# Rounding and clipping by a signed-byte write in the quantised feed-forward of a gated cross-attention block

## The reference

```python
def _act_fake_quant(x, clip_factor):
    scale = sigmoid(clip_factor) * max(abs(x)) / 127
    return clip(round(x / scale), -128, 127) * scale

xq = _act_fake_quant(layernorm(x), clip_x)
h  = _act_fake_quant(silu(xq @ Wg.T) * (xq @ Wu.T), clip_down)
x  = x + tanh(g_ffn) * (h @ Wd.T)          # Wg, Wu, Wd rounded by rows in the same manner
```

## Time and profile before

| | |
|---|---|
| median of 3 runs | 256.78 us (256.52 to 256.97) |
| span of the profiled execution, first to last instruction | 255.8 us; no time of its own is shown for this execution |
| median less span | 0.95 us, what lies around the span |
| PE busy | 212.0 us (83%), 1661 instructions |
| DVE busy | 217.3 us (85%), 447 instructions |
| ACT busy | 163.1 us (64%), 300 instructions |
| POOL busy | 137.8 us (54%), 241 instructions |
| granted TensorE clock, mean | 0.964 of full speed |

### The profile page before, as it was taken

The page is one execution under the profiler, slowest core; times in us unless marked ns, Lnnn a source line. Parts: engine busy times, 40 slices in busy tenths (PEclk is TensorE's granted clock), DMA queues, the critical chain, the costliest instruction groups (busy, mean ns, idle before and its releaser), DMA issues.

```text
span 255.8 us, 5381 instructions
## 1 busy us (share of the span) xinstructions
PE 212.0 (83%) x1661; PEld 144.3 (56%) x1664; DVE 217.3 (85%) x447; ACT 163.1 (64%) x300; POOL 137.8 (54%) x241
## 2 busy tenths in 40 slices
PE   0899999979989999999999999988672979846860
PEld 0688888857746666666656666644341433314640
DVE  3377799979898998989989898969977999999991
ACT  2246666475687766666677766677664778839920
POOL 7445568643452536284774848388835533320671
PEclk9999999999999999999999999999995899995996
DMA  6998959999446444355445252000003200000594
GB/s 221 236 293 285 295 142 233 275 256 256 133 151 165 141 110 104 95 118 128 125 111 136 55 136 64 4 0 4 1 0 108 100 1 0 0 1 0 65 137 133
DMA packets 34185, 30.80 MB, mean 120 GB/s; under 512 B 5232, under 2 KB 27760, under 8 KB 34160
## 3 DMA queue, kind: packets, MB, share of 16 engines
q1 hardware_dynamic: 29776, 27.74, 39.7%
q0 software_dynamic: 1360, 1.31, 4.2%
q10 hardware_dynamic: 3024, 1.44, 2.1%
HBM read 20.65 MB, written 9.70 MB: 119 GB/s over the span
## 4 chain that ended last, share of the span: by engine, by line
PE 34%; DVE 30%; issue 10%; ACT 7%; POOL 7%; DMA 5%; SPq 4%; POOLq 0%; ACTq 0%; DVEq 0%
PE bank_o L1466 9%; PE bank_a L1449 6%; PE bank_b L1435 4%; DVE h_max L1212 3%; PE bank_a L1475 3%; DVE arena L1248 3%; ACT arena L763 3%; DMA big<-in_ctx 3%; DVE big L1221 3%; PE bank_a L1352 3%; DMA big<-max_parts 2%; DVE arena L903 2%; DVE arena L1254 2%; DVE v_all L1270 2%; POOL big L485 1%
## 5 line engine op out<-in xcount | busy, mean ns | idle before, releaser
L913 DVE TENSOR_REDUCE neg_max<-bank_b 128x2 f32<-128x512 f32 x128 | 80.2, 673 | 4.9 <-PE bank_b L1341 3.0
L1449 PE MATMUL bank_a<-big 98*128 98x256 bf16 x256 | 48.9, 274 | 6.3 <-ACT arena L763 2.3
L763 ACT ACTIVATE arena<-bank_a 128x512 f32<-128x512 f32 x64 | 34.3, 605 | 13.9 <-PE bank_a L1449 13.8
L1435 PE MATMUL bank_b<-big 96*128 96x256 bf16 x224 | 42.7, 272 | 0.3 <-issue 0.2
L763 ACT ACTIVATE big<-bank_a 128x512 f32<-128x512 f32 x64 | 33.9, 595 | 12.3 <-PE bank_a L1449 12.1
L1449 PEld LDWEIGHTS bank_a<-big 98*128 98x128 bf16 x256 | 20.1, 97 | 25.5 <-issue 8.8
L1352 PE MATMUL bank_a<-arena,w_t 128*128 128x256 f32 x128 | 32.3, 401 | 0.2 <-issue 0.2
L1352 PEld LDWEIGHTS bank_a<-arena,w_t 128*128 128x128 f32 x128 | 24.7, 202 | 4.0 <-issue 0.6
L509 POOL TENSOR_TENSOR arena<-resid,arena 128x512 bf16<-128x512 f32 x16 | 18.4, 1163 | 10.9 <-ACT arena L701 10.9
L1435 PEld LDWEIGHTS bank_b<-big 96*128 96x128 bf16 x224 | 21.1, 97 | 4.5 <-issue 0.8
L569 POOL TENSOR_TENSOR x_rows<-x_rows,arena 128x256 f32<-128x256 f32 x14 | 11.6, 834 | 15.4 <-ACT arena L772 15.4
(11 more groups left out here) (179 smaller groups left out, 444.4 us busy)
## 6 DMA issues: line engine op xcount, KB each, us to landing
qk_parts<-arena SPq DMA_DIRECT2D x8, 768.0 KB, 4.9
big<-qk_parts SPq DMA_DIRECT2D x32, 192.0 KB, 3.2
big<-qk_parts SPq DMA_DIRECT2D x32, 128.0 KB, 3.2
x_rows<-in_x SPq DMA_DIRECT2D x8, 256.0 KB, 6.5
big<-qk_parts SPq DMA_DIRECT2D x32, 64.0 KB, 3.5
big<-in_ctx SPq DMA_DIRECT2D x7, 256.0 KB, 5.1
out<-x_rows SPq DMA_DIRECT2D x7, 256.0 KB, 2.8
out<-v_all POOLq DMA_DIRECT2D x5, 256.0 KB, 4.7
```

What stands on the lines that cost most here:

```text
L763: act.activation(probabilities(h), ring_bank(b, ("exp", h)).rearrange("p (c s) -> p c s", c=QC), ACT.Exp, scale=SCALE).then_inc(exp_done, 1)
L913: dve.tensor_reduce(neg_max[:, p, :, h], bank.rearrange("p (c s) -> p c s", c=QC), axis=AX.X, op=ALU.max, negate=True).then_inc(max_done, 1)
L1435: done = mm(to, q_st[0:KR, p, h, c * P:(c + 1) * P], k_st[0:KR, p, h], start=True, stop=not masked)
L1449: done = mm(to, k_st[0:KM, p, h, k * P:(k + 1) * P], q_st[0:KM, p, h], start=True, stop=not masked)
```

## The change

A write of an f32 value as a signed byte rounds it and holds it within -128 and 127. The change multiplies by the inverse scale and writes signed bytes, and a second instruction copies the bytes into bf16. The constant MAGIC, its removal and both clips go away for x and for h; the weights keep theirs. The byte buffers take a quarter of the room, so `x_int` holds all four chunks and `h_int` all eight batches, and the waits for a free buffer go away. ACT rounds h in one instruction of 128 x 768 (tile 1) and seven of 128 x 1536 (batches 1 to 7), where there were 15 of 128 x 768, and DVE copies h in two instructions of 128 x 768 and seven of 128 x 1536. The instructions before and after:

```diff
-                pool.tensor_scalar(xq[:, n % 2].rearrange("p t e -> p (t e)"), hats(n), INV_X, MAGIC, ALU.mult, ALU.add
+                pool.tensor_scalar(x_int[:, n].rearrange("p t e -> p (t e)"), hats(n), INV_X, 0.0, ALU.mult, ALU.add
                                    ).then_inc(pool_x, 1)
...
             over_scale(2)
-            pool.wait_ge(xq_ready, 3)
             over_scale(3)
...
-            act.activation(xq[:, 0, 2:4], v_all[:, 2:4], ACT.Identity, scale=INV_X, bias=magic[:]
-                           ).then_inc(x_over_scale, 1)
+            act.activation(x_int[:, 0, 2:4], v_all[:, 2:4], ACT.Copy, scale=INV_X).then_inc(x_over_scale, 1)
...
-            for t in range(1, T // P):
-                act.wait_ge(y_free, t + 1)
-                act.activation(h_round[:, t % CT], h_all[:, :, t * P:(t + 1) * P], ACT.Identity,
-                               scale=INV_H, bias=magic[:]).then_inc(y_rounded, 1)
+            act.activation(h_int[:, 0, :, P:S], h_all[:, :, P:S], ACT.Copy, scale=INV_H).then_inc(h_int_ready, 1)
+            for b in range(1, B):
+                act.activation(h_int[:, b], h_all[:, :, b * S:(b + 1) * S], ACT.Copy, scale=INV_H
+                               ).then_inc(h_int_ready, 1)
...
-            def rounded(to, rows):
-                chain.then(dve.tensor_scalar(to, rows, -MAGIC, QMAX, ALU.add, ALU.min))
-
-            def clip(to):
-                chain.wait()
-                dve.tensor_scalar(to, to, -QMAX - 1, None, ALU.max).then_inc(xq_ready, 1)
+            def whole_x(n, t=slice(0, CT)):
+                dve.tensor_copy(xq_b[:, n, t], x_int[:, n, t]).then_inc(xq_ready, 1)
 
             def quantise_ahead():
                 for n in (2, 3):
                     dve.wait_ge(pool_x, n - 1)
-                    rounded(xq_b[:, n - 1], xq[:, n % 2])
-                chain.wait()
-                for n in (2, 3):
-                    clip(xq_b[:, n - 1])
-
-            chain.step(dve.tensor_scalar(xq[:, 0, 0:2], v_all[:, 0:2], INV_X, MAGIC, ALU.mult, ALU.add))
-            rounded(xq_b[:, 0, 0:2], xq[:, 0, 0:2])
-            clip(xq_b[:, 0, 0:2])
+                    whole_x(n)
+
+            chain.step(dve.tensor_scalar(x_int[:, 0, 0:2], v_all[:, 0:2], INV_X, None, ALU.mult))
+            whole_x(0, slice(0, 2))
+            chain.step(dve.tensor_scalar(w_scale_x[:], w_scale[:, 0:2 * IC], S_X, None, ALU.mult))
             dve.wait_ge(x_over_scale, 1)
-            rounded(xq_b[:, 0, 2:4], xq[:, 0, 2:4])
-            chain.then(dve.tensor_scalar(w_scale_x[:], w_scale[:, 0:2 * IC], S_X, None, ALU.mult))
-            clip(xq_b[:, 0, 2:4])
-            chain.step(dve.tensor_scalar(xq[:, 1].rearrange("p t e -> p (t e)"), hats(1), INV_X, MAGIC, ALU.mult, ALU.add))
-            dve.wait_ge(xq_tr, 2)
-            rounded(xq_b[:, 0], xq[:, 1])
-            clip(xq_b[:, 0])
+            whole_x(0, slice(2, 4))
+            chain.step(dve.tensor_scalar(x_int[:, 1].rearrange("p t e -> p (t e)"), hats(1), INV_X, None, ALU.mult))
+            whole_x(1)
             dve.wait_ge(pad_zero, 2)
...
-            chain.step(dve.tensor_scalar(h_round[:, 0], h_all[:, :, 0:P], INV_H, MAGIC, ALU.mult, ALU.add))
+            chain.step(dve.tensor_scalar(h_int[:, 0, :, 0:P], h_all[:, :, 0:P], INV_H, None, ALU.mult))
+            dve.tensor_copy(hq[:, :, 0:P], h_int[:, 0, :, 0:P]).then_inc(hq_ready, 1)
+
             def whole(b):
-
-                def round_tile(i):
-                    if i:
-                        dve.wait_ge(y_rounded, i)
-                    dve.tensor_scalar(hq[:, :, i * P:(i + 1) * P], h_round[:, i % CT], -MAGIC, None, ALU.add
-                                      ).then_inc(y_free, 1)
-
-                def clip_tile(i):
-                    t = slice(i * P, (i + 1) * P)
-                    dve.wait_ge(y_free, i + CT + 1)
-                    dve.tensor_scalar(hq[:, :, t], hq[:, :, t], QMAX, -QMAX - 1, ALU.min, ALU.max
-                                      ).then_inc(hq_ready, 1)
-
-                i = b * QC
-                round_tile(i)
-                if b == 0:
-                    clip_tile(i)
-                round_tile(i + 1)
-                if b:
-                    clip_tile(i)
-                clip_tile(i + 1)
+                dve.wait_ge(h_int_ready, b + 1)
+                t = slice(b * S + (P if b == 0 else 0), (b + 1) * S)
+                dve.tensor_copy(hq[:, :, t], h_int[:, b, :, P if b == 0 else 0:S]).then_inc(hq_ready, 1)
...
                 def down_tile(b, c, to):
-                    pe.wait_ge(hq_ready, b * QC + c + 1)
+                    pe.wait_ge(hq_ready, b + 2 if b else c + 1)
```

More of the change, by code:

```diff
@@ L28 @@
 U8 = mybir.dt.uint8
+I8 = mybir.dt.int8
 MAGIC = 12582912.0
@@ L216, in flamingo_block @@
         p_second = part(HH * QC * S).rearrange("p (h c s) -> p h c s", h=HH, c=QC)
-        xq = part(2 * CT * E, True).rearrange("p (a t e) -> p a t e", a=2, t=CT)
-        xq_b = part(3 * CT * E // 2).bitcast(BF16).rearrange("p (a t e) -> p a t e", a=3, t=CT)
+        x_int = part(NCH * CT * E // 4, True).bitcast(I8).rearrange("p (a t e) -> p a t e", a=NCH, t=CT)
+        xq_b = part(NCH * CT * E // 2).bitcast(BF16).rearrange("p (a t e) -> p a t e", a=NCH, t=CT)
         xq_t = part(EC * T // 2).bitcast(BF16).rearrange("p (c t) -> p c t", c=EC)
@@ L222, in flamingo_block @@
         up_scaled = part(CW)
-        h_round = wgu_rows[:].rearrange("p g c e -> p (g c e)").rearrange(
-            "p (a c t) -> p a c t", a=CT, c=IC)
+        h_int = wgu_rows[:].rearrange("p g c e -> p (g c e)").bitcast(I8).rearrange(
+            "p (b c t) -> p b c t", b=B, c=IC)
         hq = part(IC * T // 2, True).bitcast(BF16).rearrange("p (c t) -> p c t", c=IC)
@@ L282, in flamingo_block @@
         pad_zero, h_scale_ready = sem("pad_zero"), sem("h_scale_ready")
-        y_rounded, y_free, hq_ready = sem("y_rounded"), sem("y_free"), sem("hq_ready")
+        h_int_ready, hq_ready = sem("h_int_ready"), sem("hq_ready")
         down_done, y_scaled, x2_stored = sem("down_done"), sem("y_scaled"), sem("x2_stored")
@@ L883, in _ @@
             dve.memset(ones_f[:], 1.0).then_inc(consts, 1)
-            for s, n in ((res_done, 2), (v_stored, 1), (h_done, 2), (pool_h_done, 1), (up_copied, 1), (y_free, CT), (y_scaled, 4)):
+            for s, n in ((res_done, 2), (v_stored, 1), (h_done, 2), (pool_h_done, 1), (up_copied, 1), (y_scaled, 4)):
                 dve.sem_inc(s, n)
@@ L1551, in feed_forward, with xq_transpose @@
                 pe.wait_ge(wd_scale_ready, 1)
-                def xq_transpose(n, buffer):
+                def xq_transpose(n):
                     pe.wait_ge(xq_ready, n + 2)
@@ L1557, in xq_transpose @@
                         for t in range(CT):
-                            done = tr(bank[:, k * CW + t * P:k * CW + (t + 1) * P], xq_b[:, buffer, t, k * P:(k + 1) * P],
+                            done = tr(bank[:, k * CW + t * P:k * CW + (t + 1) * P], xq_b[:, n, t, k * P:(k + 1) * P],
                                       ident_b[:])
@@ L1604, in gate_up @@
                         if ahead and c == 2:
-                            xq_transpose(n + 1, n)
+                            xq_transpose(n + 1)
                 first_product()
```

## The result

The changed kernel takes 255.08 us in the median of 20 runs, the kernel before, run beside it, 257.33 us. The ratio is 0.9894 (95% interval 0.987 to 0.9918), so 2.7 us less (2.1 to 3.3). The medians are over all 20 runs of each kernel and lie only 2.25 us apart; the ratio leaves out the executions of either kernel that fell into a slower state of the chip. The forecast was 4.6 us less (252.2 us, own range 251.2 to 253.2, whole range 250.8 to 256.3). The direction and the whole range held; the time lies outside the own range of the likeliest case.

A forecast was written before the change was run, and what follows sets the result against it. VectorE was taken to bound the changed part, the last 60 us. Span 255.8 - 3.0 (down stage) - 1.6 (x) = 251.2 us; with the median 0.95 above the span, 252.2 us, own range 251.2 to 253.2, whole range 250.8 to 256.3.

The forecast's parts named there:

- What a byte costs VectorE: VectorE's byte passes in both rounding stages: bytes run at the middle pace, 0.51 ns per element, with 0.98 as the other end.
- Rival (b): VectorE's byte copies run at the slow pace, 0.98 ns per element, making the kernel slower, 258.1 us; chance 0.16.
- ScalarE by batches: ScalarE's rounding of h: a batch of 1536 lasts 1.56 us and the next starts after 1.47; upper bound 1.84.
- Rival (c): ScalarE gains nothing from rounding h in batches, 1.84 us for 1536; 253.5 us in all, up to 256; chance 0.07.
- TensorE's slow start decides here: Down stage: half-clock matmuls until 236.6 us make TensorE finish at 245.1, later than VectorE and ScalarE allow.
- The period I gave VectorE: Rounding h: VectorE's time per batch falls from 2.08 to 1.47 us, a copy of 0.87 replacing 1.48.
- issues take 1.43 to 1.49 us amid such passes: GpSimd's accumulating stores before the change: issue times read as showing little of VectorE locking GpSimd out.
- The last tiles "by 246.8 (0.35 + 1.04, as now)": End of the down stage: tile 15 is scaled and added by 246.8 us, against 250.61 before, 3.8 us less.
- I give back 0.4 us for crowding: Down stage: allowance for five 256 KB stores every 1.48 us, asking 177 GB/s of a queue that moved 128.
- rival (a): Accumulating stores become the bound, 2.16 us each: 1.1 us less in the down stage, 2.7 in all, 254.1 us; chance 0.17.
- the down stage: Kernel's last part, from rounding h to the final stores: forecast to take 3.0 us less.
- Rounding x, 1.6 us less: x part: one copy replaces subtraction and clip, the second product starts 2.1 us earlier; 1.6 us less, 1.2 to 2.0.

## Why the prediction was right and where it failed

**What a byte costs VectorE: right.** 0.51 ns per element, for reads and writes. Rival (b), the slower side, is out. The Trainium skill's rule (VectorE: DVE Perf Modes, "What auto-detection actually checks") that the two-port mode asks nothing of the element's size agrees with it.

**ScalarE by batches: right** (1.56 us). Rival (c) is out.

**"TensorE's slow start decides here": wrong.** At full clock from the first matmul VectorE ended at the same 17.9 us behind the scale of h. (The half clock also lasted to about 237.5 us before, not 236.6: the mean of the stretch from 236.6 to 240 is 0.87.) The period I gave VectorE, 1.47 us, held only for the first batches; from the second issue on, a copy took 1.16 to 1.19 us, since GpSimd's back-to-back issuing holds it (0.95 without the stores, 0.94 where the issues stood apart). I had read "issues take 1.43 to 1.49 us amid such passes" as a sign of little interference. Before, the issues had 0.3 to 0.6 us of idle time between them; in the change they have none.

**The last tiles "by 246.8 (0.35 + 1.04, as now)": wrong, by 1.8 us.** In the clock of the trace before, VectorE ended at 248.6. The stretched copies make up about 0.7 of it. The rest is the hold by GpSimd's adds: the 1.04 that I took over as the cost of an add was itself a held one (0.42 when free), and so was the 0.67 of tile 14. Together they had lost 0.9 us before, and they lose 2.2 in the change, where tile 14's takes 2.59. The case with the adds out of PSUM shows that cause, and that this loss hid behind another.

**"I give back 0.4 us for crowding": the mechanism of rival (a), which I had at 0.17, was at work, in part.** The queue needs 2.1 us a store, and issuing the last one 3.0 us sooner made it land 0.6 us sooner. It sets the end together with the stores behind it: a VectorE 0.7 or 2.2 us earlier gave 0 to 0.3 us, within the spread of stretch h, and dropping the five stores 2.1 (22.4 to 20.3). But stretch h came out at 22.7 and not at the 24.1 of (a), because the first issue came sooner (6.2 us behind the scale of h instead of 7.2) and the plain stores, which (a) put behind the queue, ran mostly beside it. Taken together, the down stage gave 1.8 us in the mean of the profiles (2.5 in the one pair), for the forecast 3.0, and by other limits than named.

**"Rounding x, 1.6 us less": the step that failed.** The mechanism was right: 1.9 us at full clock. I had taken ScalarE's silus as 0.4 us earlier without asking at which clock TensorE would feed them; the one that the second product waits for came 0.6 us later. In the profile before, the half clock ended at 199.9 us, 4.6 us behind the scale of x; after, at 203.6 us, 7.1 behind it, and the whole gain went into one idle microsecond and the waits behind it: the second product started 1.0 us sooner behind the scale of x instead of 2.1, and the maximum of h came at the same 34.0. Seven profiled executions with the new x part and no added matmuls gave stretches of 34.0, 34.2, 32.8, 33.0, 33.6, 33.9 and 34.0 us, 33.6 in the mean, against 34.0 to 34.3 in three with the old part. So 0.5 us is what it yields on the average of these, in line with the 0.5 of the run with the x part alone. Why the rise falls early in one execution and late in another is open.

The sum then reads: 1.8 (h) and 0.5 (x) make 2.3 us by the profiles, against 2.7 (2.1 to 3.3) measured, where 3.0 and 1.6 were forecast. That rival (a) had named just 2.7 us is luck: it put 1.1 us on the h part and 1.6 on the x part.

## What to carry to other kernels

A copy from bytes to bf16 in SBUF costs VectorE what one f32 pass costs, so a rounding by the write pays where it replaces a subtraction and a clip. When the engine that was the limit gets faster, work out again every pair that shares something: here VectorE's passes and GpSimd's issues and adds, and a queue whose service time per store was already as long as the old period. And where a gain rests on TensorE answering quickly behind an idle gap, cost it at both clocks. Before a stage is costed from one profile, ask how much the same stage differs between executions: stretch h differed by 1.4 us in three profiles with the same rounding, and VectorE's end in it by 0.1.

## What the runs showed of the hardware

- An add with both operands in SBUF stood for 2.59 us beside two adds of GpSimd, and took 0.42 with one operand in PSUM. A byte copy of 0.95 us took 2.94 beside GpSimd's adds and 1.17 beside its back-to-back issuing of stores, while an issue took up to 2.6 us for 1.49 before. The Trainium skill (SBUF — State Buffer, "SBUF: two separate sides") names a lock that VectorE and GpSimd share, in which whoever starts first makes the other wait for the whole instruction. The copy beside the adds agrees with it (it ended its own 0.8 us of streaming behind them). The issuing does so only in part: it cost a copy 0.2 us, and issues of 1.20 us that stood apart overlapped copies of 0.94 at no cost to either.
- Five accumulating stores of 256 KB took 2.1 us each of all sixteen DMA engines (the time of their packets, summed) whether issued 2.07 or 1.5 us apart; plain stores of the same size took under 1 us (6.1% and 1.3% of 31 us for 0.79 MB).
- The same four plain stores, issued at the same distances, ended the span 25.2, 24.9 and 23.8 us behind the scale of h in three executions.
- 17 added matmuls ahead of the x part kept the granted clock at 1.00 through it in four profiles, and 9 did not in one.
